# Storing the mixed tokens from ScalarE's DMA queue, behind the copies that make them, in a two-layer FFN kernel on one core

## What is computed

```python
x = x + _L0_ffn_ref(_L0_cond_ref(x, cond, L0_weight, L0_c_weight, fside), L0_ffn_weight)
x = x + _L1_ffn_ref(_L1_cond_ref(x, cond, W0, b0, W1, b1, W2, b2, weight, bias_k), W, b, A, Bmat, LiMEs)
...
def _L0_cond_ref(x, c, weight, c_weight, bias):      # grouped 9-tap convolution along the positions
    out = lax.conv_general_dilated(x, weight, ..., feature_group_count=4)
    return out + ctx[:, :, None] + bias[None, :, None]
def _L0_ffn_ref(input_act, weight):                  # int8 rows times int8 weight, 1024 x 1024
    x_q, w_q = round(input_act / a_scale), round(weight / w_scale)
    return (x_q @ w_q.T) * a_scale * w_scale.T
def _L1_cond_ref(x, embedding, ...):                 # per batch a 64 x 64 mix of the channels
    out = jnp.einsum('boi,bih->boh', agg_w, x) + agg_b[:, :, None]
def _L1_ffn_ref(x, W, b, A, Bmat, LiMEs):            # dense 1024 x 1024, plus a gated rank-32 term
    return x @ W.T + b + (z * p_mix) @ Bmat * scaling
```

## Time and profile before

| | |
|---|---|
| time, median of 3 runs | 612.7 us (612.19 to 615.58) |
| profiled execution | 613.3 us, span 611.5 us |
| PE busy | 604.1 us (99% of the span) |
| DVE, POOL, ACT busy | 433.3, 375.0, 357.0 us (71, 61, 58%) |
| granted TensorE clock | 0.999 of full speed |
| bytes moved by DMA | 136.24 MB, mean 223 GB/s |

### The profile page before, as it was taken

How to read it: one execution, slowest core, us unless ns; L and a number is a source line. 1 busy time by engine, 2 the same in 40 slices (tenths; PEclk the granted TensorE clock), 3 DMA queues, 4 the chain that set the end, 5 groups by cost and what they waited for, 6 DMA issues and landing times.

```text
span 611.5 us, 16208 instructions
## 1 busy us (share of the span) xinstructions
PE 604.1 (99%) x6500; PEld 343.7 (56%) x6500; DVE 433.3 (71%) x883; ACT 357.0 (58%) x622; POOL 375.0 (61%) x252
## 2 busy tenths in 40 slices
PE   8999999999999999999999999999999999999998
PEld 5756667667776777765554444444444444444444
DVE  5988999978899999986877757754635454355543
ACT  3799998989999999876535234453233333321100
POOL 3436545546777666554888945989777659656200
PEclk9999999999999999999999999999999999999999
DMA  8989987878889999684183125765445445542111
GB/s 338 357 268 311 366 317 277 295 261 307 318 315 333 323 336 312 232 293 140 66 305 116 34 71 201 284 234 192 159 172 185 153 169 216 207 147 94 70 69 70
DMA packets 38632, 136.24 MB, mean 223 GB/s; under 512 B 5036, under 2 KB 5580, under 8 KB 38513
## 3 DMA queue, kind: packets, MB, share of 16 engines
q1 hardware_dynamic: 33518, 118.43, 54.6%
q10 hardware_dynamic: 5040, 16.78, 6.8%
HBM read 87.95 MB, written 47.24 MB: 221 GB/s over the span
## 4 chain that ended last, share of the span: by engine, by line
PE 87%; DVE 1%; issue 1%; ACT 0%; DVEq 0%
PE ps L908 42%; PE ps L612 16%; PE ps L517 9%; PE ps L709 7%; PE ps L596 4%; PE ps L890 2%; PE ps L581 2%; PE ps L657 2%; PE ps L652 1%; PE ps L621 1%; PE ps L625 0%; PE ps L692 0%; DVE yb L1459 0%; PE ps L677 0%; ACT zT L1096 0%
## 5 line engine op out<-in xcount | busy, mean ns | idle before, releaser
L612 PE MATMUL ps<-wqT,yq_both 128*128 128x512 bf16 x512 | 122.4, 379 | 0.3 <-DVE yb L1459 0.3
L1284 POOL TENSOR_TENSOR x<-x_in,f_all 128x512 f32<-128x512 f32 x64 | 74.3, 1162 | 51.1 <-DVE f_all L1496 51.0
L1288 POOL TENSOR_TENSOR x_split<-x_ph,x_split 128x1032 f16<-128x1032 f32 x25 | 53.7, 2148 | 55.5 <-ACT x_split L994 55.5
L1021 ACT ACTIVATE yv<-yb,yinv 128x128 f32<-128x128 f32 x256 | 77.8, 388 | 0.0
L1323 POOL TENSOR_TENSOR ring<-ring 128x512 f32<-128x512 f32 x56 | 72.8, 1300 | 4.3
L612 PEld LDWEIGHTS ps<-wqT,yq_both 128*128 128x128 bf16 x512 | 45.5, 99 | 46.3 <-issue 1.4
L517 PE MATMUL ps<-x_split,conv_h 128*64 128x256 f16 (+1 forms) x1248 | 60.0, 275 | 0.0
L1496 DVE SCALAR_TENSOR_TENSOR f_all<-ps,tok_scale,wsc_b 128x512 f16<-128x512 f32 x64 | 47.9, 749 | 16.7 <-PE ps L612 15.6
L517 PEld LDWEIGHTS ps<-x_split,conv_h 128*64 128x64 f16 (+1 forms) x1248 | 47.5, 108 | 9.7 <-issue 7.9
L1817 DVE SCALAR_TENSOR_TENSOR x_in<-ps,unscale,x_in 128x512 f32<-128x512 f32 x30 | 22.5, 750 | 39.9 <-PE ps L908 39.9
L1817 DVE SCALAR_TENSOR_TENSOR wst<-ps,unscale,wst 128x512 f32<-128x512 f32 x27 | 20.2, 750 | 36.7 <-PE ps L908 36.7
(11 more groups left out here) (351 smaller groups left out, 1321.5 us busy)
## 6 DMA issues: line engine op xcount, KB each, us to landing
x_in<-in_x SPq DMA_DIRECT2D x32, 512.0 KB, 6.0
x_scratch<-x SPq DMA_DIRECT2D x32, 512.0 KB, 3.7
x_ph<-in_x_phases SPq DMA_DIRECT2D x31, 516.0 KB, 5.2
x_scratch<-ring SPq DMA_DIRECT2D x26, 512.0 KB, 5.0
ring<-x_scratch SPq DMA_DIRECT2D x26, 512.0 KB, 5.2
x_in<-x_scratch SPq DMA_DIRECT2D x12, 512.0 KB, 3.5
out<-x_in ACTq DMA_DIRECT2D x12, 512.0 KB, 3.5
wst<-in_w_rows SPq DMA_DIRECT2D x10, 512.0 KB, 6.7
```

The lines of the kernel that those rows point to most:

```text
L612: last = mm(acc_bank(t, h), yqT[:, t % 2, p, :], wqT[:, p, h * HALF:(h + 1) * HALF], start=p == 0, stop=p == PH - 1)
L1021: last = A(yv[:, s, :], yb[:, t % 2, s, :], ACT.Copy, scale=yinv[:, s:s + 1], bias=MAGIC)
L1284: g.tensor_tensor(x1[:, t % 2, s], x_in[:, t % 3, s], f16[:, s], ALU.add).then_inc(sem("x1_ready"), 1)
L1288: g.tensor_tensor(x_split[:, (t - SPLIT) % 2, 1, :], phases(t), x_split[:, (t - SPLIT) % 2, 0, :], ALU.subtract).then_inc(sem("xl_ready"), 1)
```

## The change

`save_x2` moves from SP's list to ACT's. SP issued the store of tile c-4 in step c, between `save_x1(c-3)` and `load_x(c)`. Now ACT issues the store of tile c-3 in step c, directly ahead of `tokens_sb(c-1)`, behind the ACTIVATEs that stand between the two `high` copies and `tokens_sb`; for tile 0 it stands behind `tokens_sb(2)`. The wait for `hi_ready`, the bytes, the addresses and the semaphore that the store raises stay as they were. `SAVED` is 26, so there are 26 such stores.

```diff
@@ the SyncE block @@
-            def save_x2(t):
-                wait(sp, "hi_ready", 2 * t + 2)
-                sp.dma_start(x2_dram[t], ring[:, t % RING, :]).then_inc(sem(f"x2_moved{t % RING}"), 16)
-
...
                 if c >= 3:
                     save_x1(c - 3)
-                if c >= 4 and c - 4 < SAVED:
-                    save_x2(c - 4)
@@ the ScalarE block @@
+            def save_x2(t):
+                act.wait_ge(sem("hi_ready"), 2 * t + 2)
+                act.dma_start(x2_dram[t], ring[:, t % RING, :]).then_inc(sem(f"x2_moved{t % RING}"), 16)
+
...
                     high(0, 0)
                     high(0, 1)
                     tokens_sb(2)
+                    save_x2(0)
                     row_sums(0)
                     continue
...
+                if c - 3 < SAVED:
+                    save_x2(c - 3)
                 tokens_sb(c - 1)
```

## The result

The changed kernel is slower: 623.2 us (median of 6 runs, 619.52 to 881.24) against 613.04 us for the kernel before (6 runs beside it, 612.19 to 615.58). The ratio is 1.0147 [1.0119, 1.0175]. The profiled execution took 622.12 us, with a span of 620.3 us: 8.8 us more than before.

What follows compares the result with a forecast made beforehand. The prediction took PE as the bound, with little room on ACT. All terms were 0, so 613.3 us profiled stayed, less 0.6 us for the median of runs: 612.7 us, range 610.7 to 615.5.

Steps and rivals of the forecast that it cites:

- rival 2: PE's odd gaps in the first stage go or grow with another queue mix: 610.7 or 614.7 us; chance 0.15.
- The list of what would show the prediction wrong: ACTq issues above 1.5 us with growing PE idle time, ACT idling for `x_ph`, or PE's unexplained gaps vanishing, over 3 us.
- a small tail: Outcomes of PE's odd gaps beyond 0.5% on both sides; upper tail and scatter of runs together got 0.02.
- What the transfers do: First-stage store leaves 2.7 us sooner against the phases' load, delaying it at most 1.6 us of 10.4 allowed; cost 0.
- rival 1: ACT's issue of the first-stage store stalls; at 1.8 us per issue +10 us, 623; chance 0.08.
- PE "for all 50.00 us": PE was busy for the whole window from 200 to 250 us, so PE was taken as the bound.
- ACT's price is 0: The store's issue on ACT, 0.34 to 0.44 us, hides beneath a running ACTIVATE; cost 0, at most +1.0 us.
- SP's freed time: SP loses 26 issues, some 11 us or more; its waits for x1 grow instead; worth 0.
- Rivals 1, 3 and 4: ACT's issue stalls, 0.08; phases landing late for ACT, +28 us, 0.02; earlier loads freeing PE, at most 2.81 us faster, 0.04.
- The Trainium skill's rule: DMA engines alternate between queues packet by packet; the store takes up to half the rate, phases lose about 1.6 us.

Runs made afterwards that it cites:

- g1: The changed kernel, store still early on ACT, with SP's load of the phases moved behind its save of x1: 614.54 us, ratio 1.0025.
- g2: The kernel before, with SP issuing the store early, then x1's save, then the phases' load: 614.33 us, ratio 1.0025.
- e5: The changed kernel with each store cut to 64 of 1024 columns (32 KB), the second stage reading x1's tiles instead: 612.07 us, ratio 0.9989.
- e6: The kernel before plus a useless 256 KB store on ACT at the changed kernel's places: 620.38 us, ratio 1.0139.
- e7: The kernel before with the store on SP put last in the step, behind all loads: 616.73 us, ratio 1.0052.
- e8: The kernel before with 32 one-column matmuls added at the start of PE's list: 619.07 us, ratio 1.0103.
- e1: The kernel before with SP's store issued ahead of x1's save in the same step: 620.5 us, ratio 1.0102.

## Why the prediction was wrong

**The step that failed** is rival 2's size: "Doubling it gives 614.7. Both are within 0.5%." Its mechanism, an instruction load held up by data, with "another mix of queues can move it", is what happened, except that the mix of bytes in time moved it and not the queues. The bound was not worked out from anything that limits the stops. It took the idle time of one window for all there could be (of its 2.03 us only 1.20 us is such a stop), and twice that for the worst. The stops grew fourfold, 2.0 to 8.2 us, and behind one of them the clock fell, which the sum had no term for: 6.2 and some 1.7 us of the 8.8 us, instead of at most 2.0. The list of what would show the prediction wrong had these gaps only for the better. Its chance of 0.15, "half each way", had nearly all of the answer in what I called "a small tail".

**What the transfers do, "cost: 0"**, was right in each sentence and wrong in its scope. No wait for the phases shows up and nobody waits for the store. But only readers of data were counted. PE's instructions are a consumer of DMA too, and I had its 52 transfers in the earlier trace rows.

**The lull.** Under rival 1 the store "comes in a lull of SP's list" stood as a point in favour, since ACT's issue wouldn't stall there. That lull is what was spent. With it gone the DMA engines had no free slice ahead of PE's densest group, and giving it back by another way, in g1, took the ratio from 1.0147 to 1.0025.

**PE "for all 50.00 us"** from 150 to 250 us was read as a proof that there is nothing to lose there except by ACT. It only shows that every instruction came in time under the old order.

**Right.** ACT's price is 0: 26 issues of 0.326 to 0.346 us, issued at 147.24, 0.03 us after the copies' end at 147.21 (146.15 + 1.06), with `tokens_sb` starting 0.09 us behind its neighbour, as in the kernel before. ACT's busy time is the same but for 0.7 us. SP's freed time is worth 0 and went into its wait for x1, 110.8 to 124.1 us. Rivals 1, 3 and 4 didn't come about: no issue on ACT was long, no engine waited for the phases' load, and nothing got faster.

**The Trainium skill's rule** of "DMA: Bandwidth & Descriptors", section "Queues, rings and completion order", as the prediction cites it, changed nothing in the sum: the place of the bytes in time decides, while g1 and g2, with two queues and with one, take 614.54 and 614.33 us.

**Open.** When PE asks for a load, and so whether it is the request or something before the packet that waits: the packets themselves took no longer in a long stop (0.96 us against 0.95). That they begin later in PE's list is in the traces, and that bytes in the pause bring this about follows from e5, e6 and g1; what holds them back there isn't recorded. Open too are 0.9 us of the sum, e7's 5.0 us, part of e8's time, and why g1 stays 0.25% above the kernel before although its stops are as short; its 2.3 us of late phases may be the reason, which no run tests. None of these kernels is faster than the kernel before. e5, without any stop and with 480 KB less to store for each tile, has a ratio of 0.9989 with 1 inside its interval [0.9973, 1.0005]: by that, removing every stop would be worth 1.7 us at most.

## What to carry to other kernels

Where a busy engine's time is 99% and its program is long and unrolled, count its instruction loads among the readers of DMA, and look at the idle time "<- issue" amid a group of equal instructions before moving any transfer; it can grow by more than a factor of two. A lull in the DMA shares just ahead of a dense group of small instructions is a resource: before moving half a megabyte into one, look at what else lives from it. When a store must move there, move another transfer out, and measure both together.

## What the runs showed of the hardware

- PE's instruction loads are 16 KB each; the packet ahead of a stop took 0.88 to 1.67 us, and PE resumed 1.2 to 1.6 us after it had landed, in all 54 stops. The Trainium skill's page "Runtime: NRT & Kernel Launch", section "Instruction fetch mechanics", gives blocks of 16 KiB, 256 instructions, for the refill of an engine's instruction memory, and calls the cost of crossing a boundary mostly hidden. The size agrees with the rows. So does "mostly" by number, since 45 of the changed kernel's 52 loads stop nothing in the mix; but the other seven cost 8.2 us.
- Stops grew when 512 KB or 256 KB were stored ahead of them, up to 2.85 us for one (in e1), and were gone when it was 32 KB instead of 512 KB.
- The clock isn't tied to the length of a stop alone: it fell to 0.50 for 3.4 us behind one of 2.33 us here, and behind two of 2.24 and 2.15 us in e1, but not behind e1's of 2.85 us, nor behind this one in e6:

```profile
223.76 0.58 PE L597 MATMUL ps<-mix_home,x 64*64 64x64 f32 x24 [2.40 <-issue]
```

- Executions of one kernel scatter together with these falls: 617.7 us at a mean clock of 1.000 and 623.5 us at 0.995, of the same program.
